# Windowed attention with a router behind it: one reciprocal for both tiles of a chunk, statistics ahead of their joins, and another order of TensorE's step

## What is computed

```python
x = x + _layernorm(_L0_attn_ref(_layernorm(x), w_lin))        # heads 16, window 31
# _L0_attn_ref: softmax over 31 taps per head, then out[t] = sum_k w[t,k] * xh[t-30+k]
x = x + _layernorm(_L0_ffn_ref(_layernorm(x), ...))           # router logits: yn @ gate_w.T
```

## Time and profile before

| | before |
|---|---|
| median of 3 runs | 1059.19 us (1057.85 to 1061.36) |
| profiled execution, its own time | 1060.0 us |
| its span, first to last instruction | 1058.0 us |
| PE busy | 949.1 us, 90% |
| DVE busy | 844.8 us, 80% |
| POOL busy | 583.6 us, 55% |
| ACT busy | 555.7 us, 53% |
| mean granted clock of PE | 0.961 of full speed |
| product phase of half 0, alone | about 94 to 185 us |
| product phase of half 1, to the block end | about 273 to 395 us |

### The profile page before, as it was taken

How to read it: one execution, slowest core, us unless ns; L and a number is a source line. 1 busy time by engine, 2 the same in 40 slices (tenths; PEclk the granted TensorE clock), 3 DMA queues, 4 the chain that set the end, 5 groups by cost and what they waited for, 6 DMA issues and landing times. The chain is left out here.

```text
span 1058.0 us, 27078 instructions
## 1 busy us (share of the span) xinstructions
PE 949.1 (90%) x9256; PEld 834.2 (79%) x9257; DVE 844.8 (80%) x2274; ACT 555.7 (53%) x1314; POOL 583.6 (55%) x843
## 2 busy tenths in 40 slices
PE   4997899899789849999999799999999989899994
PEld 3766788788778748778788799899998777788884
DVE  5987998788899758888886488788887588787877
ACT  5994355799345433344334555555555344445543
POOL 4451555522255510378873466566562788888873
PEclk9998999899999959999999899999999899999997
DMA  5532578733368741122222455555556666655652
GB/s 169 178 92 68 168 216 254 227 124 100 77 186 232 232 141 47 57 79 85 86 90 75 94 177 172 170 165 170 164 176 136 206 197 190 189 165 169 189 164 90
DMA packets 155795, 157.91 MB, mean 149 GB/s; under 512 B 52528, under 2 KB 135600, under 8 KB 155696
## 3 DMA queue, kind: packets, MB, share of 16 engines
q1 hardware_dynamic: 137648, 113.98, 34.9%
q0 software_dynamic: 13056, 35.67, 12.5%
q10 hardware_dynamic: 4992, 6.95, 2.3%
HBM read 91.90 MB, written 64.63 MB: 148 GB/s over the span
## 5 line engine op out<-in xcount | busy, mean ns | idle before, releaser
L830 POOL DMA_INDIRECT xg<-yn_scratch,ids x144 | 136.9, 951 | 106.4 <-PE bank L1215 73.8
L1365 POOL DMA_INDIRECT cy<-expert_rows,slots x128 | 142.9, 1116 | 54.2 <-issue 35.6
L777 PE MATMUL bank<-yh,gh 128*128 128x512 f32 x352 | 142.0, 403 | 16.5 <-PEq L164 7.9
L661 PE MATMUL bank<-xbd,am 128*32 128x68 f32 x4096 | 138.3, 304 | 11.0 <-DMA xbd<-xn_scratch 6.7
L777 PE MATMUL bank<-yh,gl 128*128 128x512 f32 x352 | 141.6, 402 | 0.0
L777 PE MATMUL bank<-yl,gh 128*128 128x512 f32 x352 | 141.5, 402 | 0.0
L661 PEld LDWEIGHTS bank<-xbd,am 128*32 128x32 f32 x4096 | 122.9, 128 | 18.5 <-issue 8.8
L934 POOL TENSOR_SCALAR in_row<-col,row_f 128x128 bf16<-128x128 bf16 x128 | 97.0, 775 | 66.4 <-DVE row_f L1037 39.6
L1239 PE MATMUL bank<-eh,xh 128*128 x288 | 93.8, 326 | 0.6 <-DVE xl L1283 0.6
L777 PEld LDWEIGHTS bank<-yh,gh 128*128 128x128 f32 x352 | 67.9, 193 | 31.2 <-issue 14.8
L1283 DVE TENSOR_TENSOR xl<-bank,xh 128x256 fp32r<-128x256 f32 x144 | 61.1, 425 | 34.7 <-ACT xh L1265 27.2
(11 more groups left out here) (191 smaller groups left out, 2896.1 us busy)
## 6 DMA issues: line engine op xcount, KB each, us to landing
expert_rows<-yo SPq DMA_DIRECT2D x144, 128.0 KB, 1.9
xbd<-xn_scratch SPq DMA_DIRECT2D x128, 72.0 KB, 2.4
xt<-xp SPq DMA_DIRECT2D x32, 256.0 KB, 2.7
xn_scratch<-xn SPq DMA_DIRECT2D x64, 128.0 KB, 2.7
xr<-x SPq DMA_DIRECT2D x32, 256.0 KB, 3.6
x_scratch<-x SPq DMA_DIRECT2D x32, 256.0 KB, 3.4
yn_scratch<-yn SPq DMA_DIRECT2D x32, 256.0 KB, 4.5
ynt_scratch<-ynt SPq DMA_DIRECT2D x32, 256.0 KB, 4.7
```

Of the source, the lines that this page charges most:

```text
L661: ins = nc.tensor.matmul(pso[q][t][J * b:J * b + J, g * MW:(g + 1) * MW], am[:, q, g, e, side], xbd[:, q, e + side, :, g], start=(g == 0 a ...
L777: ins = self.nc.tensor.matmul(self.pb[2 * k + half][:], w[:, c, col:col + P], y[:, n % 2, c, :], start=(j == 0), stop=(j == 5))
L830: return nc.gpsimd.indirect_dma_start(out=to, out_offset=None, in_=yn_d.rearrange("n p c -> (n p) c"), in_offset=bass.IndirectOffsetOnAxis ...
L1365: nc.gpsimd.indirect_dma_start(out=y[:, r, t, j], out_offset=None, in_=yg_d, in_offset=bass.IndirectOffsetOnAxis(ap=slots[:, 2 * unit + t, ...
```

## The change

Four edits, all in `attention`. `divided` makes one reciprocal over both tiles, which lie in two neighbouring PSUM banks (for this the eight banks become one tensor). The joins leave `divided` and `moments3` and become functions of their own, `joined` and `joined3`, which DVE calls after both sets of statistics. PE's step becomes router, `turn_yn`, then both halves of the products. And the logits of all chunks but six (those of half 0 whose router runs among taps steps) go to banks 4 and 5 in turn instead of the bank that `turn_yn` writes, so that `turn_yn` waits for the copy of the logits only behind those six and the first.

```diff
+        ROUTED = 6
+        def apart(n):
+            return n >= NCH or n + ROUTED < NCH
+        def logits_place(n, t):
+            if apart(n):
+                return pb[4 + n % 2][:, t * C:t * C + GW]
+            return psy[t][:, 0:GW]
...
             def divided(n):
                 q = n % 2
-                for t in range(2):
-                    m = n * 2 + t
-                    pv = pso[q][t][:, 0:NG * MW].rearrange("p (g w) -> p g w", g=NG)
-                    ve.wait_ge(s["pso_full"], n + 3)
-                    nc.vector.reciprocal(rs[:, t].rearrange("p (k g) -> p g k", g=NG),
-                                         pv[:, :, SLOT_C:MW]).then_inc(s["rs_ok"], 1)
-                    ve.wait_ge(s["rs_ok"], m + 1)
+                pv = banks[:, 2 * q:2 * q + 2, 0:NG * MW].rearrange("p t (g w) -> p t g w", g=NG)
+                ve.wait_ge(s["pso_full"], n + 3)
+                nc.vector.reciprocal(rs[:].rearrange("p t (k g) -> p t g k", g=NG), pv[:, :, :, SLOT_C:MW]).then_inc(s["rs_ok"], 1)
+                ve.wait_ge(s["rs_ok"], n + 1)
+                for t in range(2):
                     nc.vector.tensor_tensor(
...
-                for t in range(2):
-                    m = n * 2 + t
-                    wait_apart(ve, s["ve_passed"], s["st2_ok"], m + 1)
-                    nc.vector.bn_aggr(mv2[:, q, t], st2[:, q, t]).then_inc(s["mv2_ok"], 1)
+
+            def joined(n):
+                for t in range(2):
+                    wait_apart(ve, s["ve_passed"], s["st2_ok"], n * 2 + t + 1)
+                    nc.vector.bn_aggr(mv2[:, n % 2, t], st2[:, n % 2, t]).then_inc(s["mv2_ok"], 1)
...
+            def joined3(n):
                 for t in range(2):
                     wait_apart(ve, s["ve_passed"], s["st3_ok"], n * 2 + t + 1)
                     nc.vector.bn_aggr(mv2[:, n % 2, 2 + t], st3[:, n % 2, t]).then_inc(s["mv3_ok"], 1)
...
                 at(h, i - 1, divided)
                 at(h, i - 2, moments3)
+                at(h, i - 1, joined)
+                at(h, i - 2, joined3)
...
             def turn_yn(n):
...
                     pe.wait_ge(s["yn_ok"], m + 5)
-                    pe.wait_ge(s["lg_ok"], n * 2 + 2)
+                    if n > 0:
+                        pe.wait_ge(s["ynt_ok"], n * 2)
+                    if n == 0 or not apart(n - 1):
+                        pe.wait_ge(s["lg_ok"], n * 2 + 2)
...
             def product_step(h, i):
-                at(h, i - 6, router)
+                at(h, i - ROUTED, router)
+                at(h, i - 5, turn_yn)
                 at(h, i, lambda n: products(n, 0))
-                at(h, i - 5, turn_yn)
                 at(h, i, lambda n: products(n, 1))
```

More of the change, by code:

```diff
@@ L71, in build_program @@
         block_expert = sb("block_expert", [1, NBK + 12], I32)
-        pb = [ctx.enter_context(nc.psum_tensor(f"bank{i}", [P, 512], F32)) for i in range(8)]
+        banks = ctx.enter_context(nc.psum_tensor("bank", [P, 8, 512], F32))
+        pb = [banks[:, i] for i in range(8)]
         top = TopTwo(nc, logits, sb, ctx.enter_context(nc.semaphore("top_step")))
@@ L81, in build_program @@
                   rows.put("yl", [P, 2, CC, 512], F32R, 16384))
-        attention(nc, x, xp, wd, gw, wsh, wdn, split, raw, rows, sems, turned, xn_d, yn_d, ynt_d, x2_d, ident, ones, neg_half, eps, logits, top, pb)
+        attention(nc, x, xp, wd, gw, wsh, wdn, split, raw, rows, sems, turned, xn_d, yn_d, ynt_d, x2_d, ident, ones, neg_half, eps, logits, top, banks, pb)
         so = sb("so", [P, 4, C])
@@ L157, in skewed, with attention @@
         step(i, i % 2)
-def attention(nc, x, xp, wd, gw, wsh, wdn, split, raw, rows, sems, turned, xn_d, yn_d, ynt_d, x2_d, ident, ones, neg_half, eps, logits, top, pb):
+def attention(nc, x, xp, wd, gw, wsh, wdn, split, raw, rows, sems, turned, xn_d, yn_d, ynt_d, x2_d, ident, ones, neg_half, eps, logits, top, banks, pb):
     x_blk = xp.rearrange("(h u) (b j) c -> h (u b) j c", h=HALVES, j=J)
@@ L450, in divided @@
                 q = n % 2
+                pv = banks[:, 2 * q:2 * q + 2, 0:NG * MW].rearrange("p t (g w) -> p t g w", g=NG)
+                ve.wait_ge(s["pso_full"], n + 3)
+                nc.vector.reciprocal(rs[:].rearrange("p t (k g) -> p t g k", g=NG), pv[:, :, :, SLOT_C:MW]).then_inc(s["rs_ok"], 1)
+                ve.wait_ge(s["rs_ok"], n + 1)
                 for t in range(2):
-                    m = n * 2 + t
-                    pv = pso[q][t][:, 0:NG * MW].rearrange("p (g w) -> p g w", g=NG)
-                    ve.wait_ge(s["pso_full"], n + 3)
-                    nc.vector.reciprocal(rs[:, t].rearrange("p (k g) -> p g k", g=NG),
-                                         pv[:, :, SLOT_C:MW]).then_inc(s["rs_ok"], 1)
-                    ve.wait_ge(s["rs_ok"], m + 1)
                     nc.vector.tensor_tensor(
                         av[:, q, t].rearrange("p (k g r) -> p g k r", k=HS, g=NG),
-                        pv[:, :, 0:SLOT_C].rearrange("p g (k r) -> p g k r", k=HS),
+                        pv[:, t, :, 0:SLOT_C].rearrange("p g (k r) -> p g k r", k=HS),
                         rs[:, t].rearrange("p (k g) -> p g k", g=NG)[:, :, :, None].to_broadcast([P, NG, HS, HC]),
@@ L463, in divided @@
                 for t in range(2):
-                    m = n * 2 + t
-                    ve.wait_ge(s["av_ok"], m + 5)
+                    ve.wait_ge(s["av_ok"], n * 2 + t + 5)
                     nc.vector.bn_stats(st2[:, q, t], av[:, q, t]).then_inc(s["st2_ok"], 1)
+            def joined(n):
                 for t in range(2):
-                    m = n * 2 + t
-                    wait_apart(ve, s["ve_passed"], s["st2_ok"], m + 1)
-                    nc.vector.bn_aggr(mv2[:, q, t], st2[:, q, t]).then_inc(s["mv2_ok"], 1)
+                    wait_apart(ve, s["ve_passed"], s["st2_ok"], n * 2 + t + 1)
+                    nc.vector.bn_aggr(mv2[:, n % 2, t], st2[:, n % 2, t]).then_inc(s["mv2_ok"], 1)
             def moments3(n):
@@ L546, in put_logits @@
                     act.wait_ge(s["psg_full"], n * 2 + 2)
-                    nc.scalar.activation(logits[:, m:m + 1, :], psy[t][:, None, 0:GW], ACT.Copy).then_inc(s["lg_ok"], 1)
+                    nc.scalar.activation(logits[:, m:m + 1, :], logits_place(n, t)[:, None, :], ACT.Copy).then_inc(s["lg_ok"], 1)
             def centred(n):
@@ L599, in product_step @@
             def product_step(h, i):
-                at(h, i - 6, put_logits)
+                at(h, i - ROUTED, put_logits)
                 at(h, i - 2, centred)
@@ L680, in router @@
                 pe.wait_ge(s["ynt_ok"], n * 2 + 2)
+                if n > 1:
+                    pe.wait_ge(s["lg_ok"], n * 2)
                 for t in range(2):
                     for c in range(CC):
-                        ins = nc.tensor.matmul(psy[t][:, 0:GW], ynt[:, n % 2, t, c], gws[:, c, :],
+                        ins = nc.tensor.matmul(logits_place(n, t), ynt[:, n % 2, t, c], gws[:, c, :],
                                                start=(c == 0), stop=(c == CC - 1))
```

## The result

The changed kernel takes 1094.91 us (median of 4 runs, 1092.59 to 1096.07) against 1060.28 us for the kernel before on the same chips; the ratio is 1.0327 with a 95% interval of 1.03 to 1.0354. It is slower by 34.6 us, where the forecast was 1094 us and 34.9 us more. The profiled execution took 1092.59 us, its span is 1090.7 us.

What follows compares the result with a forecast made beforehand. A closed circle of POOL and ACT was taken to set the 5.81 us step. Half 0 16.5, half 1 18.8 and end -0.4 make 34.9 us on 1060.0: 1094.9, stated as 1094 us; range 1077 to 1108.

Steps and rivals of the forecast that it cites:

- the circle of POOL and ACT: Product phase before the change: scales, `centred`, `normal2`, `residual` wait on each other in a closed loop of 5.79 us, the step's length.
- Its two terms: Per masked step: 0.91 us for POOL's wait through DVE's moved joins, 0.61 us for masking holding POOL's scales; 1.52 us together.
- The hold of the masking: POOL's scales, held up by DVE's masking instructions, take 2.68 instead of 2.07 us: 0.61 us more per step.
- the third case: Rival: masking holds L350 as well as L351; scales take 3.19 us, 2.03 us more per step, 1105 us; chance 0.13.
- the forecast's case: In POOL's scales L350 reads just ahead of the masking and L351 is held; scales 2.68 us, 1094 us; chance 0.58.
- the rival with two held: Masking holds both L350 and L351 in POOL's scales: 2.03 us more per step, 1105 us; chance 0.13.
- The rival by which the scales slip through: L351 gets past the masking, so only 0.94 us per step remain (0.91 + 0.03): 1081 us; chance 0.17.
- The covered edits: One reciprocal on DVE and PE's new order gain nothing in steady steps; uncovered, the reciprocal would be worth 8 us.
- half 0's hidden load: Step from 178.02, where POOL's taps step waited for a load of `x`, hides the longer step: 0.5 us back.
- the steps without masking: Half 1's two steps with no masking behind the scales take 6.36 instead of 5.45 us each: 1.8 us more.
- the first steps: At the start of each half, where POOL waits for DVE anyway: 0.3 us more per half.
- the end: After half 1's products, ACT's `turned_out` no longer waits for transposes held by the logits' copy: 0.4 us gained once.

## Why the prediction was right

**The circle.** The step on which everything rested, that the moved joins put DVE into the circle of POOL and ACT, is shown by the rows of the changed kernel (DVE idle 2.00 us for `x2`, forecast 1.9; POOL idle for the join), and by the two runs that undo and that make this one edit.

**Its two terms** were mis-sized, in opposite directions, and nearly cancel: 1.65 and 1.60 us per step measured over the two halves, 1.52 forecast. The way from `residual`'s end to the scales takes 0.69 us, not 0.87, so that the wait is 0.73 us more per step instead of 0.91. All of the difference lies in its last part: from the first join to the scales are 0.31 us (142.72 to 143.03), not 0.49. The rows of before that gave 0.49 us were joins that follow the statistics of their own tile directly; in the changed order those are long done, and a pair of joins takes 0.23 us instead of 0.41. So the moved joins do get shorter, at a place that DVE now waits at.

**The hold of the masking** was forecast as 0.61 us, with 1.12 as the case in which L350 is caught too; it is 0.97. The same reading of the joins is behind it. The 0.33 us that the prediction took for each pair is the distance from a pair to the statistics behind it in the old order; in the new one the pairs start 0.15 us apart (142.72 and 142.87) and the masking 0.18 us later, 0.02 us behind the scales' start instead of 0.17. So L360 (once L350) is caught, as in the third case. The third case's 3.19 us of scales become 3.04 since the maskings begin, and end, 0.15 us sooner; in both L365 (once L355) starts behind the last of them.

So the steady steps are not the forecast's case, in which one operation is held, but that of the rival with two held, which got a chance of 0.13 and 1105 us; the long L360 is the sign that the prediction named for it. That the time falls within 1 us of the forecast's is in part luck: the wait was priced some 0.18 us too high and the hold 0.36 us too low. What the prediction had right is the mechanism: a circle closed through DVE, and POOL held by the masking that the moved joins bring closer to it.

A step in which the joins happened to take longer shows the forecast's own case. The timelines of DVE and of POOL in the changed kernel:

```profile
172.60 0.47 DVE L478 BATCH_NORM_AGGREGATE mv<-st 128x2 f32<-128x6 f32 x2
173.03 0.32 DVE L489 BATCH_NORM_AGGREGATE mv<-st 128x2 f32<-128x6 f32 x2
173.27 2.46 DVE L454 TENSOR_TENSOR am<-probs,mask 128x512 f32<-128x512 f32 x4
```

```profile
173.15 0.20 POOL L360 TENSOR_TENSOR rstd<-mv,eps 128x4 f32<-128x4 f32 x1 [0.93 <-DVE mv L478]
173.30 0.68 POOL L361 TENSOR_TENSOR shift<-zero,mv 128x4 f32<-128x4 f32 x1
174.07 1.34 POOL L363 TENSOR_TENSOR rstd<-rstd,neg_half 128x4 f32<-128x4 f32 x1
175.48 0.31 POOL L365 TENSOR_TENSOR shift<-shift,rstd 128x4 f32<-128x4 f32 x1
```

With the masking 0.12 us behind the scales L360 slips through, L361 is held, and the scales take 2.64 us; forecast were 2.68. By the prediction's estimate, a read 0.15 us after the start, L360 would have been held here as well; it slips through at 0.12 us, and at 0.13 in the step at 309.89.

**The rival by which the scales slip through** (1081 us) fell. The Trainium skill, page "SBUF — State Buffer", section "Who interferes with whom", says that whichever issues first gets the shared pair of ports. In the trace L360 starts at 143.03, ahead of the masking at 143.05, and is held for all of that instruction. So the start that a trace shows does not decide by itself: here a POOL operation of 0.20 us that was 0.02 us ahead was held, and one that was 0.12 us ahead, in the step above, was not. That the other then waits until the instruction ends agrees with the rows above (0.74 us for L360, 0.65 for L361).

**The covered edits.** One reciprocal and PE's order were put at nothing, with DVE's and PE's spare time as the cover. In the changed kernel DVE waits 2.2 us and PE 1.8 us in a step, and without the moved joins all three remaining edits are worth 0.2%. With the cover gone they are worth 4.6 us together (1056.83 to 1052.23), where 8 us were given for the reciprocal alone: the double one takes 0.35 us against twice 0.25, so that 0.15 us of work and some waits are saved, 0.20 us of DVE's step (5.64 to 5.44), and PE's 5.63 us then limit what it gives. The remaining small terms: half 0's hidden load -0.5 (measured -0.7), the steps without masking +1.8 (+1.4, again for the shorter joins), the first steps +0.3 each (+0.2 and +0.5, from the first scales of a half to those of step 3), the end -0.4 (-0.6).

## What to carry to other kernels

Before an instruction is moved behind others on an in-order engine, ask what those others wait for: here two short joins, moved behind two statistics that wait for POOL's `residual`, closed a circle over three engines. Look for circles by adding the rows from one start of an operation to its next; where the sum is the step, only the arcs of that circle are worth work, and an edit beside it (one reciprocal less, a better order on PE) shortens the step only once the circle is cut, which took a third buffer here. When a moved instruction shifts what runs beside what, price the meeting too: here it cost 0.97 us a step, the wait 0.73.

## Not expected

PE's clock fell in some steps of the changed kernel, which the prediction had only among its "something else" (0.04), and the products did not mind. The windows view of the changed kernel (start and end in us, length, busy time of PE, PEld, DVE, ACT, POOL, granted clock, DMA share, GB/s), and PE's timeline:

```profile
163.70:166.00 2.30, 2.30 (x12) 1.97 (x12) 1.64 (x7) 0.26 (x2) 1.61 (x3) 0.61 0.50 106
166.00:168.00 2.00, 2.00 (x65) 2.00 (x68) 2.00 (x5) 0.00 (x0) 1.92 (x3) 0.59 0.92 251
168.00:170.20 2.20, 2.20 (x72) 1.94 (x64) 1.60 (x5) 1.69 (x4) 0.40 (x2) 1.00 0.72 250
```

```profile
163.70 1.44 PE L700 MATMUL bank<-gws,ynt 128*128 128x18 f32 x8 [1.56 <-ACT ynt L585]
164.98 1.09 PE L689 MATMUL bank<-ident,yn 128*128 128x128 f32 x4
166.01 4.23 PE L673 MATMUL bank<-xbd,am 128*32 128x68 f32 x128
```

The granted clock is 0.61 and 0.59 over the first two stretches, mostly the 1.2 GHz level, and back at 1.00 in the third. PE had idled 1.56 us before. The length of that idle time does not tell alone: behind 1.79 us the clock stayed at 1.00 over PE's work from 141.30, behind 1.82 and 1.80 us it was 0.70 and 0.71 over that from 148.77 and from 156.23. What else decides is not shown here. The transposes take 1.09 us instead of 0.64, but the 128 small products 4.23 instead of 4.17. PE ends at 170.24 and then waits another 0.94 us for ACT, so the lower clock does not set this step.
